# A two-attention transformer block: cross attention opened on batch 0, query projections moved into its first group, head exchange without HBM, feed-forward norms on ScalarE

## What is computed

```
B, T, S, C, H, D = 2, 1024, 77, 256, 16, 16
xn1 = ln(x) * g1 + be1
x = x + mha(xn1, xn1, causal=True) @ W1 + b1      # self attention
xn2 = ln(x) * g2 + be2
x = x + mha(xn2, ctx, causal=False) @ W2 + b2     # cross attention, 77 keys
xn3 = ln(x) * g3 + be3
out = x + relu(xn3 @ Wf1 + bf1) @ Wf2 + bf2       # 256 -> 1024 -> 256
# mha: scores = (q @ k.T) * sqrt(D), softmax over keys, @ v, 16 heads of 16
```

## Time and profile before

| what | value |
|---|---|
| median of 3 runs | 616.51 us (613.1 to 619.86) |
| profiled execution | 614.4 us, of it a span of 612.6 us |
| granted TensorE clock, mean of the span | 0.897 of full |
| busy: PE, DVE, ACT, POOL | 82%, 55%, 51%, 30% |
| chain that ended last: PE, DMA, DVE, ACT | 52%, 19%, 11%, 7% |
| DMA traffic | 56.51 MB |

### The profile page before, as it was taken

One profiled execution on the slowest core, in us unless ns is written; L12 is line 12 of the kernel. 1 busy time (PEld: TensorE's weight loads), 2 busy tenths in 40 slices (PEclk: granted clock), 3 DMA queues, 4 the chain that ended last, 5 costly groups with the idle time before them and its releaser, 6 DMA issues.

```text
span 612.6 us, 8804 instructions
## 1 busy us (share of the span) xinstructions
PE 502.4 (82%) x3296; PEld 293.0 (48%) x3296; DVE 335.8 (55%) x653; ACT 313.5 (51%) x606; POOL 183.3 (30%) x284
## 2 busy tenths in 40 slices
PE   1588875999998999999887478568886667989887
PEld 1386642444443444343433154334323357988877
DVE  3166985787787886878420246445231753454431
ACT  3685313686776775767566303346451534253460
POOL 2598940222221223131325303214140540121200
PEclk9999995999999999999999976757555968999999
DMA  8045954062829084818610483879333112101001
GB/s 291 37 143 183 191 147 77 1 92 50 137 72 144 2 139 95 119 16 87 175 40 34 118 156 79 136 109 173 106 112 106 70 43 67 35 0 36 18 17 35
DMA packets 42890, 56.51 MB, mean 92 GB/s; under 512 B 13024, under 2 KB 29152, under 8 KB 42848
## 3 DMA queue, kind: packets, MB, share of 16 engines
q1 hardware_dynamic: 40544, 47.56, 38.0%
q10 hardware_dynamic: 2304, 8.39, 4.0%
HBM read 35.12 MB, written 20.42 MB: 91 GB/s over the span
## 4 chain that ended last, share of the span: by engine, by line
PE 52%; DMA 19%; DVE 11%; ACT 7%; SPq 4%; POOL 3%; issue 2%; ACTq 0%; DVEq 0%
PE ps L907 12%; PE ps L996 10%; PE ps L1021 9%; PE ps L959 8%; DMA stacks<-shift_t 6%; PE ps L1108 5%; DMA arena_h<-heads 5%; DMA recips<-recip_rows 4%; DVE max_a L1187 4%; ACT arena_p L765 3%; PE ps L891 3%; DMA heads<-out_t 2%; PE ps L981 2%; SPq L442 2%; SPq L414 2%
## 5 line engine op out<-in xcount | busy, mean ns | idle before, releaser
L765 ACT ACTIVATE arena_p<-ps 128x512 f32<-128x512 f32 (+4 forms) x416 | 190.2, 542 | 121.8 <-PE ps L996 119.5
L1187 DVE TENSOR_REDUCE max_a<-ps 128x1 f32<-128x512 f32 (+4 forms) x280 | 159.2, 619 | 51.7 <-PE ps L959 38.9
L996 PE MATMUL ps<-stacks 99*128 99x512 bf16 (+2 forms) x448 | 149.2, 366 | 28.9 <-DMA stacks<-shift_t 23.7
L959 PE MATMUL ps<-stacks 96*128 96x77 bf16 (+4 forms) x640 | 142.5, 300 | 13.3 <-DVE max_a L1187 10.2
L959 PEld LDWEIGHTS ps<-stacks 96*128 96x128 bf16 x640 | 58.5, 111 | 77.8 <-DVE max_a L1187 36.6
L1021 PE MATMUL ps<-arena_p,v_group 128*32 128x512 f32 (+4 forms) x896 | 94.1, 540 | 0.7 <-POOL arena_p L639 0.5
L639 POOL TENSOR_SCALAR_AFFINE_SELECT arena_p<-arena_p 128x512 f32<-128x512 f32 x64 | 41.0, 653 | 163.8 <-ACT arena_p L765 163.8
L996 PEld LDWEIGHTS ps<-stacks 99*128 99x128 bf16 (+1 forms) x448 | 45.2, 107 | 93.5 <-ACT arena_p L765 37.3
L1187 DVE TENSOR_REDUCE max_b<-ps 128x1 f32<-128x384 f32 (+3 forms) x88 | 52.5, 635 | 19.7 <-PE ps L963 19.7
L907 PE MATMUL ps<-wf2r,hid_r 128*128 128x256 f32 x384 | 48.6, 289 | 9.2 <-DVE hid_r L1300 9.2
L907 PEld LDWEIGHTS ps<-wf2r,hid_r 128*128 128x128 f32 x384 | 47.8, 197 | 10.4 <-DVE hid_r L1300 10.4
(11 more groups left out here) (70 smaller groups left out, 534.9 us busy)
## 6 DMA issues: line engine op xcount, KB each, us to landing
heads<-out_t ACTq DMA_DIRECT2D x16, 512.0 KB, 4.0
stacks<-qc_parts SPq DMA_DIRECT2D x48, 128.0 KB, 5.0
stacks<-q_parts SPq DMA_DIRECT2D x42, 128.0 KB, 4.9
stacks<-k_parts SPq DMA_DIRECT2D x42, 128.0 KB, 7.4
arena_h<-heads SPq DMA_DIRECT2D x8, 512.0 KB
recips<-recip_rows SPq DMA_DIRECT2D x8, 512.0 KB
q_parts<-parts SPq DMA_DIRECT2D x8, 384.0 KB, 2.6
k_parts<-parts SPq DMA_DIRECT2D x8, 384.0 KB, 2.8
```

Source lines behind the costliest of these rows:

```text
L765: nc.scalar.activation(probs[0:a.kp, a.probs_slot(g, ui), h, k * BANK:k * BANK + width], ps[0:a.kp, unit % S_BANKS, 0:width], ACT.Exp, sca ...
L959: ins = nc.tensor.matmul(m_bank(use)[:, o:o + w], q_stack[0:ROWS, g % a.nb, h, t * P:(t + 1) * P], k_rows(ROWS, g, h, s0, s0 + w), start=T ...
L996: ins = nc.tensor.matmul(ps[0:keys, unit % S_BANKS, lo - k * BANK:hi - k * BANK], k_rows(ROWS_S, g, h, i * P, i * P + keys), q_stack[:, g ...
L1187: nc.vector.tensor_reduce(dst, m_bank(use)[:, 0:nh * w].rearrange("p (h w) -> p h w", h=nh), AX.X, ALU.max).then_inc(s.max_read, 1)
```

## The change

Five things change together.

1. **Cross attention opens on batch 0.** SP stores units 0 to 3, loads the stacks of groups 0 and 1 and runs the first 12 entries of the list (through the shift of group 0) before it loads groups 2 and 3. PE runs the eight chunks of group 0 straight behind the output projections, then turns norms 6 and 7.
2. **Batch 1's four query projection units become entries of the list** inside cross group 0, with a `second` entry (ACT's second part) and a `third` entry (POOL's third part, SP's store) for each. At the last one SP waits until all have landed and loads group 4. The ring of three PSUM banks for chunks now serves them too.
3. **Heads go from SBUF to SBUF.** No HBM tensor and no `store_out`: per group one DMA moves the sums (`pack_sums`) and four the heads (`pack_heads`), on SP; for the last group ACT issues the sums. The steps of the exchange stand elsewhere in the list: for self `inverted`, `stored`, `spread` at unit 15 instead of 31 and `divided` at 31 instead of 43; for cross two groups behind instead of three.
4. **Loads of later stacks are spread**, one DMA per score entry of the next group, and cross has `lead` 1.8 for 2.3 and `gap` 0.25 for 0.5.
5. **Norms 8 and 9 are applied by ACT** (two more small POOL instructions each), biases of chunks 0 to 3 are added during cross groups 1 to 4, and in the feed-forward part the output projection of chunk n + 2 stands before `feed_out(n)`. DVE's `invert_sums(7)` stands before `xn_low_half(0)`.

```
-            ends = [max(u ...) for step in (2, 3, 3, 3, 5)]     # loaded, inverted, stored, spread, divided
+            ends = [max(u ...) for step in (1, 1, 1, 3)]        # inverted, stored, spread, divided
-            self.moves = {"loaded": (2, 4), "inverted": (3, 0), "stored": (3, 1), "spread": (3, 3), "divided": (3, 6)}
+            self.moves = {"inverted": (2, 0), "stored": (2, 1), "spread": (2, 2), "divided": (2, 7)}
+        self.packed = 2 * GH if causal else GH
-CROSS = Attention(False, S_CTX, buffers=5, lead=2.3, gap=0.5, rows=...)
+CROSS = Attention(False, S_CTX, buffers=5, lead=1.8, gap=0.25, rows=...,
+                  projected=[(0.05, 0.2, 0.35), (0.2, 0.35, 0.5), (0.35, 0.5, 0.65), (0.5, 0.65, 0.8)])
+        def pack_sums(eng, s, g):
+            eng.wait_ge(s.out_copied, g + 1)
+            at_least(eng, s.recips_stored, 16 * (g // 2))
+            eng.dma_start(sums[r0:r0 + GW, :], out_t[D::2 * D, :]...).then_inc(s.sums_in, 16)
+        def pack_heads(eng, s, g):
+            eng.wait_ge(s.out_copied, g + 1)
+            for h in range(GH):
+                eng.dma_start(heads_out[r0 + h * D:r0 + (h + 1) * D, g // 2, :],
+                              out_t[2 * D * h:2 * D * h + D, :]).then_inc(s.heads_in, 16)
...
# SP, per entry of the list
+                    if op == "third":
+                        u = U_QC + NCH + what[0]
+                        store_parts(u)
+                        if u + 1 == U_H:
+                            wait_parts(U_H)
+                            load_stacks(CROSS, S2, 4)
+                    if op == "score" and what[1] == a.packed and what[0]:
+                        pack_sums(sp, s, what[0] - 1)
+                        pack_heads(sp, s, what[0] - 1)
+                    if op == "score" and what[0] and what[1] in a.load_at:
+                        load_stacks(a, s, what[0] - 1 + a.nb, [blk])     # one of its DMAs
...
# SP, between the attentions
+            for u in range(U_QC, U_QC + NCH):
+                store_parts(u)
+            wait_parts(U_QC + NCH)
+            load_stacks(CROSS, S2, 0)
+            load_stacks(CROSS, S2, 1)
+            attention(CROSS, S2, 0, CROSS_EARLY[1])
+            load_stacks(CROSS, S2, 2)
+            load_stacks(CROSS, S2, 3)
+            attention(CROSS, S2, CROSS_EARLY[1])
...
# PE
+            attention(CROSS, S2, 0, CROSS_EARLY[0])
             turn_norm(NCH + 2)
-            qc(2)
-            attention(CROSS, S2, 0, CROSS_EARLY[0])
             turn_norm(NCH + 3)
-            attention(CROSS, S2, CROSS_EARLY[0], CROSS_EARLY[1])
-            qc(3)
-            attention(CROSS, S2, CROSS_EARLY[1], -1)
+            attention(CROSS, S2, CROSS_EARLY[0], -1)
...
# feed-forward, PE, for each n
-                feed_out(n)
                 if n + 2 < NCH:
                     heads_product(2 * NCH + n + 2, S2, W2)
+                feed_out(n)
...
# ACT, end of cross: exp 7.4, norm 8, exp 7.5 to 7.7, copy_out(6), norm 9, then
                     copy_norm(2 * NCH)
                 copy_out(NG - 1)
-                store_out(NG - 1)
+                pack_sums(act, s, NG - 1)
...
# DVE, behind the cross list
-            if NG - 3 in CROSS.left("inverted"):
-                invert_sums(NG - 3)
+            invert_sums(NG - 1)
             xn_low_half(0)
```

More of the change, by code:

```diff
@@ L128, in use @@
         def use(what):
-            if what[0] == "norm":
+            if what[0] in ("norm", "second", "third"):
                 self.pe.append(what)
@@ L148, in order @@
         self.use_at = {what: i for i, what in enumerate(self.uses)}
+        self.read_by = [0]
+        for what in self.uses:
+            self.read_by.append(self.read_by[-1] + (what[0] != "qc"))
     def unit_width(self, u):
@@ L476, in attention @@
                         load_shift(a.uses[what[0]][1])
-                    if op == "score" and a.behind("loaded", *what) is not None:
-                        load_heads(a.behind("loaded", *what))
+                    if op == "third":
[7 more added lines that the diff above has]
+                        pack_heads(sp, s, what[0] - 1)
                     if op == "score" and a.behind("stored", *what) is not None:
@@ L692, in _ @@
             ln_root(NCH + 3)
[L693 to L696 removed]
+            attention(CROSS, S2)
             pool.wait_ge(S2.pv, CROSS.n_steps * NG)
```

210 lines of the change are left out of this document (102 added, 108 removed).

## The result

| | median of the runs | range, runs |
|---|---|---|
| before, same chips | 614.81 us | 612.68 to 619.86, 4 |
| after | 622.41 us | 617.29 to 626.41, 4 |

The ratio is 1.0122, 95% interval 1.0072 to 1.0172: 1.2% slower, where 12 us less was forecast. All ratios and intervals of this document leave out executions over 1.5% above the fastest of the same kernel; the medians and ranges have them all. The profiled execution of after took 617.29 us, the fastest of its four, with a span of 615.5 and a mean clock of 0.892, against 614.4 and 612.6 before. So the traces show 2.9 us of the 7.6 by which the medians differ.

A forecast was written before the change was run, and what follows sets the result against it. Bounds were seen in shifts behind other DMAs, the serial head exchange and DVE's waits for reciprocals, then PE from feed-forward on. Terms -4.3 - 21 + 15 - 0.2 - 1.6 = -12.1 gave a 604 us median; range 588 to 616.

The forecast's parts named there:

- Self attention: Self attention stage: earlier spread of reciprocals removes two shift waits, PE is then the limit; 4.3 us less.
- 1.46 us taken for the store of reciprocals: Exchange of heads: landing time of the reciprocals' store, 1.46 us, read from the end of self attention.
- Between the attentions: End of self attention to first cross score: direct exchange, earlier stacks and a shift without loads ahead; 21 us less.
- Inside cross: First cross score to first output projection: added projections and SP's queue delay shifts, groups 0, 1, 3, 5 long; 15 us more.
- 1.5 us taken off for lower traffic: Cross attention: no 512 KB stores, so faster landings; 1.5 us off the 16.5 more.
- The bound, 25 more: Upper end for cross: groups 0 and 1 at half clock, both shift landings 8.85 us; 25 us more.
- The end of cross: First output projection to first hidden matmul: GpSimd wait goes, group 7's sums DMA replaces it; 0.2 us less.
- The slower case: Rival, chance 0.1: self attention's last four stack loads land late, costing 3.6 us in each of five groups; 622 us.
- Cross keeps its pace: Rival, chance 0.2: cross stays near 73 us as DMAs land faster and loads finish before shifts; 589 us.
- Nothing gained: Rival, chance 0.1: late batch 1 stacks make cross 25 us longer, giving back the 21 us; 616 us.
- The lock rule: Rival, chance 0.05: at the end of cross, first hidden matmul follows ACT's copies, 4.6 us sooner; 599.5 us.
- The feed-forward part: Feed-forward: output projections fill PE's gaps ahead of feed_out(0) and feed_out(1), 0.7 and 0.9; 1.6 us less.

The follow-up runs named there:

- a1: Changed kernel with self attention's multiplication back at unit 43 instead of 31; 612.97 us, ratio 0.997 to before.
- d4: Kernel before with the batch 0 opening, ring projections, loads behind shifts and ACT norms; heads over HBM, old feed-forward order; 627.06 us, ratio 1.0202.
- b3: a1 with norms 8 and 9 applied by DVE again; 612.2 us, ratio 1.0012 to before.
- b2: a1 with DVE's last inversion behind its first low halves; 610.08 us, ratio 0.9967 to before.
- c3: c1 with DVE's last inversion behind the low halves of norm 8, as in b2; 600.32 us, ratio 0.9788 to before.
- d2: c2 with norms 8 and 9 applied by ACT; 597.78 us, ratio 0.9684 to before.
- c4: c2 with the changed kernel's feed-forward order, norms 8 and 9 on DVE; 604.53 us, ratio 0.9859 to before.
- b4: Kernel before with the direct exchange of heads and sums alone, cross exchange steps reordered; 605.92 us, ratio 0.989 to before.
- c2: b4 with self attention's inversion, store and spread at unit 15 and multiplication at 43; 600.34 us, ratio 0.9793 to before.
- c1: a1 with cross exchange steps reordered (store and spread at unit 4) and later cross stack loads right behind shifts; 605.56 us, ratio 0.9889 to before.
- d3: c2 run again unchanged, beside d2; 602.41 us, ratio 0.9757 to before.

## Why the prediction was wrong

- **Self attention: the step that failed.** "Self attention: 4.3 us less. ... What is late next is nothing: PE is then the limit." It measured +3.0. The working counted the spread's new place and gave the multiplication's, unit 31 for 43, no line at all. DVE waits there for a chain of 3.87 + 6.89 us. a1 undoes that one number and gives -4.9 to before: the term was right for a change that this one was not. From 97 us to the end of self attention PE waits 10.7 us for shifts and maxima before and 10.8 in after, so the step is worth the 5 us given back; the +3.0 beyond that is within what executions of the same self attention differ by. The 1.46 us taken for the store of reciprocals holds in the middle of self attention too, before the change: SP issues each spread there 1.5 us behind its store. It is 3.7 to 3.9 in two of after's three, where the change puts eight DMAs just ahead of it.
- **Between the attentions: right**, -20.3 for -21. The sums' copy landed in 2.5 us, the first score came at +41.8 for a forecast of +41.0. One step of the working did not hold: DVE's splits of units 0 to 3 end only at 351.15, the multiplication stands behind them, and the output projections start 16.9 us after the end of self attention, for 21.2 before and 13.8 forecast. So the exchange gained 4.3 us there and not 7.3. The stacks, which came at +27.9 for a forecast of +26.6, were PE's last wait ahead of the chunks (2.13 us), so the sum hardly moved.
- **Inside cross: the pattern right, the size too small**, +23.7 for +15. Group 1 was forecast by its mechanism and within 1.8 us. Group 0 was 2.8 over, 2.2 of them one wait: the working loaded groups 2 and 3 behind the first shift to free that shift and didn't ask who needs those stacks next. Group 3 was 4.5 over: 3.66 us for the store where 1.46 was kept, and a shift that landed 10.8 us after the spread's issue (430.42 to 441.21), where the earlier trace rows gave 8.55. The trace of before had a nearer price for the store: in its cross attention SP issues the two spreads 3.17 and 2.31 us behind their stores. Full groups took 9.9 us each, for 9 and 9.3. The 7.40 us of the earlier trace rows begin with the fourth score of group 2; its first stands at 414.29, so that group took 8.9. The 1.5 us taken off for lower traffic doesn't show. The bound, 25 more, held.
- **The sign.** -21 and +15 were two large terms with a difference of 6; with self attention wrong by 7.3 and cross by 8.7 there was nothing left. d4 shows that with the exchange of before this pair is a loss, 13.8 us on the way against 26.2 in cross.
- **The end of cross: right**, -0.9 for -0.2, with the sums of group 7 as the last wait. b3 shows that there ACT's norms are worth nothing, and b2, c3 and d2 what they are worth once the inversion is moved. The prediction saw that sequence and took it as given.
- **The rivals.** The slower case named 622, which is the time that came, for a cause that did not: k parts landed in 5.4 us, not in 6.8 or more, and PE did not wait for self stacks. "Cross keeps its pace" fell. "Nothing gained" had the mechanism in cross and nearly its price (23.7 of 25), but its 4.3 us of self attention were not there. The lock rule's 4.6 us did not come in after; in b2, 3.4 did, and the lock then took the low half.
- **The feed-forward part: right in sign**, -2.6 for -1.6. The working set DVE's last multiplication behind all eight low halves and gave the early inversion no part in it; c4 shows that without that inversion the order gains nothing, and PE waits 5.8 us.
- **The exchange was mis-sized.** It had 7.3 us on the way to its credit and only SP's time against it in cross. Alone (b4) it brings 2.6 on the way and 6.0 in cross, 1.1% in all, and is the gain of this change. The working priced it as waits; in b4 the gain is in PE's busy time at a higher clock, which no term of the sum had.
- **The signs.** The gap ahead of group 2 (8.09 us), the long groups 3 and 5 (20.1 and 14.3) and the inversion as the last wait came as named. The first cross score came 17.3 us sooner and not 25, by what self attention lost.

## What to carry to other kernels

Work that is pulled ahead needs its inputs ahead as well: time between two stages that looks idle on one engine may be where the next stage's loads land, and moving the start into it only moves the wait. When a step of a chain is moved earlier, look at each engine that meets it in order, not only at the one it frees, and price every DMA of it by a row from the middle of the stage, behind what is queued there. A change in five parts should be costed, and tried, part by part: here the best kernel has the exchange, the earlier self steps and the ACT norms, and the headline part costs 2% with the old exchange and shows no gain with the new one.

## What the runs showed of the hardware

**TensorE's clock made the difference between equally idle kernels.** In after PE stands 8.09 us ahead of 411.20, with the clock falling during that stall, and it then stays at the lower level through full groups. Windows of after around it:

```profile
395.45:405.60 10.15, 6.24 (x66) 3.28 (x66) 5.37 (x15) 6.81 (x13) 5.11 (x10) 1.00 0.79 198
405.60:477.20 71.60, 49.32 (x264) 20.23 (x265) 20.29 (x47) 28.46 (x46) 17.84 (x35) 0.50 0.40 70
```

For 71.6 us every window shows 0.50, also groups 2 and 4 with PE busy for 9.5 of 9.9 us. c2 and c1 do the same matmuls from the end of self attention on; their windows, way and cross, c2 first:

```profile
331.86:388.77 56.91, 36.60 (x174) 22.88 (x174) 25.59 (x60) 17.08 (x25) 19.07 (x30) 0.83 0.67 125
388.77:456.92 68.15, 46.55 (x340) 21.68 (x341) 25.70 (x62) 36.86 (x62) 19.01 (x40) 0.73 0.51 87
```

```profile
329.56:370.45 40.89, 25.98 (x141) 17.52 (x140) 20.66 (x51) 11.88 (x17) 9.99 (x14) 0.85 0.48 99
370.45:461.14 90.69, 67.07 (x372) 27.62 (x373) 34.38 (x71) 42.69 (x71) 30.22 (x57) 0.61 0.56 100
```

c2 is idle for 41.9 us and c1 for 38.5, and yet c2 is through 6.5 us sooner, because its matmuls take 83.2 us and c1's 93.1, at clocks of 0.73 and 0.61 in cross. The table says the same of all: the direct exchange without the opening has PE busy for 78 to 88 us there, every kernel with the opening for 90 to 97, and before for 94; idle are the former for 38 to 44 us, the latter for 37 to 55. The profiled executions do not stand alone in this: over the whole span every execution of b4, c2 and d3 was granted a mean clock of 0.912 to 0.934, and the 19 of before on the same chip as b4 had 0.882 to 0.916. In c2 the windows show both levels: 0.50 from 400 to 412 us, with PE busy throughout, and 1.00 from 428 to 436 and from 444 to 452. Why c2's clock comes back between stalls and after's does not is open: no run changed the pattern of stalls alone.

**A subtraction on DVE is held too**: 0.80 and 4.37 us for the same DVE instruction in b2, which the prediction looked for only in the norms.

**A small store's landing depends on its queue**: the reciprocals' store took 1.46 us alone, 3.66 to 3.87 behind four packing DMAs and three or four loads (three times in after), and 2.33 behind the packing alone (group 5 of cross in after). The Trainium skill, "DMA: Bandwidth & Descriptors", "Queues, rings and completion order", says that a semaphore increment lands only after every earlier write of the same DMA engine; these rows agree with it, and no run here isolates it.
